# Rows of 512 bytes for W and x, and half of batch 0's x transposed by VectorE

## The reference

```python
x = x + einsum('bnr,bor->bno', einsum('bni,bri->bnr', x, B0[ids]), A0[ids])   # rank 16
base   = einsum('btd,od->bto', x, W)
logits = einsum('btd,ed->bte', x, Wr) + 5.0 * one_hot(lang)
gates  = softmax over the two largest logits, 0 elsewhere
lora   = einsum('bter,bte,eor->bto', einsum('btd,erd->bter', x, A), gates, Bm)
out = x + base + 2.0 * lora
```

## Time and profile before

| | us |
|---|---|
| median of 3 runs (lowest, highest) | 1563.22 (1560.31, 1563.93) |
| profiled execution, its own time | 1561.31 |
| its span, first to last instruction | 1559.5 |
| TensorE busy | 1541.5 |
| VectorE busy | 1230.4 |
| mean granted TensorE clock | 0.996 |

### The profile page before, as it was taken

How to read it: one execution, slowest core, us unless ns; L and a number is a source line. 1 busy time by engine, 2 the same in 40 slices (tenths; PEclk the granted TensorE clock), 3 DMA queues, 4 the chain that set the end, 5 groups by cost and what they waited for, 6 DMA issues and landing times.

```text
span 1559.5 us, 20275 instructions
## 1 busy us (share of the span) xinstructions
PE 1541.5 (99%) x7430; PEld 1298.3 (83%) x7430; DVE 1230.4 (79%) x1692; ACT 714.2 (46%) x911; POOL 79.7 (5%) x119
## 2 busy tenths in 40 slices
PE   9989999999999999999999999999999999999998
PEld 8778878888888888888888888888888888888887
DVE  6998878977799767887688776997769976787665
ACT  6522222544445444455445444454444554445442
POOL 2333331000000000000000000000000000000000
PEclk9999999999999999999999999999999999999999
DMA  9899999787777767687676977667776777666564
GB/s 263 224 276 281 265 254 246 215 230 205 218 231 220 216 196 231 219 229 220 203 224 196 257 207 218 216 205 231 209 218 226 215 217 195 214 219 217 198 219 160
DMA packets 303109, 347.04 MB, mean 223 GB/s; under 512 B 204890, under 2 KB 236682, under 8 KB 302346
## 3 DMA queue, kind: packets, MB, share of 16 engines
q1 hardware_dynamic: 293602, 314.28, 69.8%
q0 software_dynamic: 9136, 30.94, 6.0%
q10 hardware_dynamic: 272, 0.52, 0.1%
HBM read 278.52 MB, written 66.72 MB: 221 GB/s over the span
## 4 chain that ended last, share of the span: by engine, by line
PE 88%; DVE 5%; SPq 4%; DMA 2%; issue 1%; ACT 0%; DVEq 0%; ACTq 0%
PE pb L804 26%; PE pb L805 26%; PE pb L806 26%; PE pb L378 4%; PE pb L380 3%; PE pb L533 2%; SPq L669 2%; SPq L292 2%; DVE raw L684 1%; DVE xl L558 1%; DMA out_dram<-ost 1%; DVE pool_a L540 1%; DMA raw<-in_L_cond_W_dram 0%; DMA an<-in_L_cond_A_dram 0%; PE pb L319 0%
## 5 line engine op out<-in xcount | busy, mean ns | idle before, releaser
L796 ACT CAST wh<-raw 128x1024 fp32r<-128x1024 f32 (+1 forms) x453 | 475.4, 1049 | 705.3 <-PE pb L806 670.9
L800 DVE TENSOR_TENSOR wl<-raw,wh 128x1024 fp32r<-128x1024 f32 (+1 forms) x453 | 552.1, 1219 | 261.3 <-ACT wh L796 260.0
L804 PE MATMUL pb<-wh,sh 128*128 128x512 f32 x1568 | 612.8, 391 | 0.5 <-DVE ost L858 0.5
L805 PE MATMUL pb<-wl,sh 128*128 128x512 f32 x1568 | 611.6, 390 | 0.0
L806 PE MATMUL pb<-wh,sl 128*128 128x512 f32 x1568 | 611.2, 390 | 0.0
L806 PEld LDWEIGHTS pb<-wh,sl 128*128 128x128 f32 x1568 | 294.3, 188 | 62.8
L804 PEld LDWEIGHTS pb<-wh,sh 128*128 128x128 f32 x1568 | 294.5, 188 | 56.2 <-DVE wl L800 0.9
L805 PEld LDWEIGHTS pb<-wl,sh 128*128 128x128 f32 x1568 | 294.6, 188 | 55.1
L378 PE MATMUL pb<-awb,xah 128*128 128x304 f32 x512 | 139.0, 305 | 0.3 <-DVE xal L355 0.3
L380 PE MATMUL pb<-awb,xal 128*128 128x256 f32 x512 | 134.6, 280 | 0.0
L804 PE MATMUL pb<-wh,xh 128*128 128x512 f32 x256 | 101.5, 396 | 0.8 <-DVE xl L558 0.8
(11 more groups left out here) (153 smaller groups left out, 1258.6 us busy)
## 6 DMA issues: line engine op xcount, KB each, us to landing
raw<-t_scr SPq DMA_DIRECT2D x392, 512.0 KB, 4.1
xst<-in_x_dram SPq DMA_DIRECT2D x448, 64.0 KB, 3.8
out_dram<-ost SPq DMA_DIRECT2D x72, 256.0 KB, 3.5
raw<-in_L_cond_W_dram SPq DMA_DIRECT2D x124, 128.0 KB, 5.3
raw<-bt_scr SPq DMA_DIRECT2D x28, 512.0 KB, 3.6
out_dram<-u SPq DMA_DIRECT2D x56, 256.0 KB, 2.9
t_scr<-raw POOLq DMA_DIRECT2D x32, 256.0 KB, 4.4
t_scr<-tst POOLq DMA_DIRECT2D x16, 512.0 KB, 6.7
```

The lines of the kernel that those rows point to most:

```text
L796: e.copy(pair_split(wh, g), pair_source(g)).then_inc(c_wh, 1)
L800: e.tensor_tensor(out=pair_split(wl, g), in0=pair_source(g), in1=pair_split(wh, g).bitcast(f32), op=ALU.subtract).then_inc(c_wl, 1)
L804: e.matmul(o, h, wh[:, g % RING, k, :], start=start, stop=False)
L805: e.matmul(o, h, wl[:, g % RING, k, :], start=False, stop=False)
```

## The change

Rows of W and of x (batches 1 to 7) in DRAM are read 128 floats at a time in place of 64. A load of W is now a "unit" of 256 output rows by 512 inputs (`unit_load`); the two units 2j and 2j + 1 together hold what `w_turn` needs for two W pieces, numbers 2j and 2j + 1, and each `w_turn` reads both. Units rotate through three places: the two `raw` places and the second half of `xst`. Batch 1's x has therefore one place (`x_block` gives `xst` half 0 while n < 2), and `x_load(e, 1, m)` waits until both units of block m - 1 have been turned. Each x block takes four DMAs instead of eight. In VectorE's list the turns of odd W pieces and the pairs of x turns stand ahead of `pair_lo`. For batch 0, blocks m = 1, 3, 5, 7 are loaded with 512-byte rows in four DMAs each and turned by VectorE (`x_turn_first`), which then copies nothing out of PSUM; TensorE keeps m = 0, 2, 4, 6, all copied by ScalarE. The tiles' order of input columns changes with it in A, A0, B0 (same count of instructions, but `columns_turn` is two transposes of half the size).

```diff
-        x_b = x.rearrange("b (h v j) (c k a n) -> b h c k a j v n", h=2, j=32, c=4, k=2, a=4)
-        def x_block(m):
-            return xst[:, m % 2, :, :].rearrange("p t n -> p (t n)")
+        x_b = x.rearrange("b (h v j) (c a n) -> b h c a j v n", h=2, j=32, c=4, a=4)
+        def x_block(n, m):
+            return xst[:, m % 2 if n > 1 else 0, :, :].rearrange("p t n -> p (t n)")
         def x_load(e, n, m, parts=range(4)):
-            if n == 1 and m < 2:
-                if 0 in parts:
+            if n and 0 in parts:
+                if n == 1 and m == 0:
                     e.wait_ge(c_bt, 4)
-            elif n and 0 in parts:
-                e.wait_ge(c_xc, 16 * (n - 1) + 2 * m - 2)
+                elif n == 1:
+                    e.wait_ge(c_xc, 2 * m)
...
-                    for k in range(2):
-                        e.dma_start(x_block(m)[32 * a:32 * a + 32, k * CW:(k + 1) * CW] ...
+                    e.dma_start(x_block(n, m)[32 * a:32 * a + 32, :].rearrange("p (v n) -> p v n", v=8),
+                                x_b[n, half, cols, a]).then_inc(d_x[m % 2 if n > 1 else 0], 16)
+        def x_turn_first(e, u):
+            if u % 2 == 0:
+                e.wait_ge(d_x0[m], 64)
+            e.transpose(two(0, q, kp)..., x_place(m)...[:, u % 2, :, :, :]).then_inc(c_x0[1], 1)
+        def unit_place(n):
+            if n in (2, 3):
+                return xst2[:, n - 2, :, :].rearrange("p t n -> p (t n)")
+            at = n if n < 2 else (n - 1) % 3
+            return (raw[:, at, :, :] if at < 2 else xst[:, 1, :, :]).rearrange("p t n -> p (t n)")
+        def unit_load(e, n):
...
+            elif n > 6:
+                e.wait_ge(c_wc, 4 * ((n - 3) // 2) + 4)
+            for a in range(4):
+                e.dma_start(unit_place(n)[32 * a:32 * a + 32, :]..., raw_w[n // 8, n % 2, n // 2 % 4, a]).then_inc(landed, 16)
         def w_turn(e, g):
-            raw_landed(e, g)
+            for n in range(w // 2 * 2, w // 2 * 2 + 2):
+                unit_landed(e, n)
         def pe_start(e):
-                if s < 12:
+                if s < 12 and (4 + s) // 2 % 2 == 0:
                     x_transpose(e, 4 + s)
         def dve_main(e):
-                if 9 <= i < 25:
-                    x_turn(e, 1, i - 9)
+                if 9 <= i < 25 and i % 2:
+                    for u in range(2):
+                        x_turn(e, 1, i - 9 + u)
+                if turns(i) and w_number(i + 3) % 2:
+                    w_turn(e, i + 3)
...
-                if i + 3 < SLOTS0 and (i + 3) % 9 != 8:
+                if turns(i) and w_number(i + 3) % 2 == 0:
                     w_turn(e, i + 3)
         def sp_main(e):
-                if 10 <= i < 22:
-                    x_load(e, 1, i // 2 - 3, (2, 3) if i % 2 else (0, 1))
-                if i + 5 < SLOTS0 and i != 3:
-                    first_load(e, i + 5)
+                if 10 <= i < 24 and i % 2 == 0:
+                    x_load(e, 1, i // 2 - 4)
+                if turns(i) and w_number(i + 3) % 2 and w_number(i + 3) >= 5:
+                    for n in range(w_number(i + 3) + 2, min(w_number(i + 3) + 4, 32)):
+                        unit_load(e, n)
```

More of the change, by code:

```diff
@@ L197, in adapted_moe_lora_kernel @@
         d_raw = [sem(f"d_raw{n}") for n in range(RAWS)]
+        d_w = [sem(f"d_unit{n}") for n in range(3)]
         d_ts, d_bs = ([sem(f"{name}{n}") for n in range(2)] for name in ("d_ts", "d_bs"))
@@ L616, in w_number @@
             return g // 9 * 8 + g % 9
-        def raw_turn(g):
-            return w_number(g) - (g > 2)
-        def raw_place(g):
-            return raw_turn(g) % 2
-        def raw_in(g):
-            return sum(32 if n == SLOTS0 - 1 else 64 for n in range(g + 1)
-                       if n != 2 and (n % 9 != 8 or n == SLOTS0 - 1) and raw_place(n) == raw_place(g))
-        def raw_before(s):
-            return raw_in(SLOTS0 - 2 + s) if s < 2 else 0
-        def raw_landed(e, g):
-            if g == 2:
-                e.wait_ge(d_w2, 64)
-            elif g in (17, 26):
-                e.wait_ge(d_btx, 32 * (g // 9))
-            else:
-                e.wait_ge(d_raw[raw_place(g)], raw_in(g))
@@ L663, in first_load @@
-            if k == 8:
-                place = btx if g in (17, 26) else raw[:, raw_place(g), 0, :]
-                for w in range(2):
-                    e.dma_start(place[:, w * HT:(w + 1) * HT], bt_scr[:, w, c * HT:(c + 1) * HT]).then_inc(landed, 16)
-            else:
-                for a in range(4):
-                    e.dma_start(w_raw(g)[32 * a:32 * a + 32, :].rearrange("p (g n) -> p g n", g=16), raw_w[c, k, a])\
-                     .then_inc(landed, 16)
+            else:
+                e.wait_ge(c_wc, 60)
@@ L674, in w_turn @@
+            for w in range(2):
+                e.dma_start(gated_place(c)[:, w * HT:(w + 1) * HT], bt_scr[:, w, c * HT:(c + 1) * HT]).then_inc(d_btx, 16)
         def w_turn(e, g):
@@ L1217, in pe_start @@
             small_transpose(e)
-            for u in range(2, 4):
-                x_transpose(e, u)
             for s in range(16):
-                if s < 12:
+                if s < 12 and (4 + s) // 2 % 2 == 0:
                     x_transpose(e, 4 + s)
@@ L1244, in act_start @@
             small_hi(e)
-            x_keep_act(e, 2)
             x_hi(e, 0, 2)
             for s in range(15):
-                if s < 12 and s % 2 == 0:
+                if s < 12 and (4 + s) // 2 % 2 == 0:
                     x_keep_act(e, 4 + s)
@@ L1282, in dve_start @@
             small_lo(e)
-            x_keep_dve(e, 3)
+            for u in (2, 3):
+                x_turn_first(e, u)
             x_lo(e, 0, 2)
             for s in range(15):
-                if s < 12 and s % 2:
-                    x_keep_dve(e, 4 + s)
+                if s < 12 and (4 + s) // 2 % 2:
+                    x_turn_first(e, 4 + s)
                 if s == 8:
@@ L1352, in pool_main, with turns @@
                     bt_difference_store(e)
+        def turns(i):
+            return i + 3 < SLOTS0 and (i + 3) % 9 != 8
         adapter = []
@@ L1389, in sp_start @@
                 e.dma_start(a0g[row:row + R, 0:D].bitcast(f32), (arh, arl)[part][0:R, :]).then_inc(d_ar, 16)
+            for n in range(4, 6):
+                unit_load(e, n)
             for s, t in enumerate((arh, arl)):
                 e.dma_start(a_scr[s, :, 0:D], t).then_inc(d_as, 16)
-            first_load(e, 4)
             e.wait_ge(c_gh, 2)
```

153 lines of the change are left out of this document (94 added, 59 removed).

## The result

The median of four runs of the changed kernel is 1612.3 us (1611.35 to 1613.01), that of the kernel before beside it 1561.76 us: a ratio of 1.0323, 95% interval 1.0305 to 1.0341. It is slower, as I said, but by 50.5 us and not by 7: far outside the range of 1557 to 1577 us that I gave.

The account below looks back on a forecast made before the run. TensorE, busy 99% of the span, was taken as the bound. Start +1.0 and loop +6.5 us on 1561.3 us gave 1568.8, or 1570.7 as a median, stated as 1570 us; range 1557 to 1577 us.

Parts of the forecast that it names:

- VectorE ... gets eight transposes: Batch 0's start: VectorE swaps eight copies of 0.60 us for eight transposes of 0.60 us, so no change.
- x turns of batches 2 to 7 cost the same: Later batches: VectorE's x turns keep their duration and wait for half as many DMAs; no loss.
- the loop's 4 x 0.60 us: Slots 9 to 23: two x turns and one w_turn on VectorE take 2.4 us of each loop.
- The start, +1.0 us, -3.8 to +3.0: Batch 0: TensorE's 3.8 us saving is lost because twelve more x DMAs delay the first W loads; +1.0 us.
- The loop, L = 13.7 us: Slots 9 to 23: turns, W and x issues and landing for batch 1's single x place take 13.7 us per two slots; +6.5 us.
- 7L - 89.4: Loop loss in us after seven loops of length L: nothing up to 12.8 us, then 0.7 us per 0.1 us.
- The output store that holds VectorE's eviction ... I keep it: Near 234 us: TensorE's 2.6 us wait for an eviction stays, between -2.6 and +1.5 us.
- columns_turn, 0.1 us, under cover: Seven times on VectorE: two half-size transposes add 0.1 us each, hidden in the main phase; 0.7 us if not.
- The gates: Batch 0: VectorE's L481 meets GpSimd's large instruction again, so TensorE's 4.4 us wait recurs.
- The clock: 100 to 120 us: granted clock stays at 0.83, 3.4 us of work lost as before; falls elsewhere would show the forecast wrong.
- What was to show it right: Low-part waits of 5 to 8 us together, x turns waiting 2 us or more, first product no earlier than 50 us.
- the lighter queue pays: Rival: halved packets land W and x sooner, start and eviction savings survive; 1556.8 us, chance 0.12.

Follow-up runs that it names:

- e8: Kernel before, with x of batches 1 to 7 and W loaded in 512-byte rows, places and order unchanged: 1562.86 us, ratio 0.9986.
- e9: e8 with one place for batch 1's x, each block requested after both turns of the block before: 1573.3 us, ratio 1.0070.
- e7: e2 with its start undone (batch 0's x in one DMA a block, transposed by TensorE alone): 1585.29 us, ratio 1.0130.
- e11: e7 with batch 0's odd blocks loaded by four DMAs each, TensorE still transposing them: 1586.32 us, ratio 1.0155.
- e2: Changed kernel with all VectorE turns reading 8 bytes apart again in place of 16: 1587.19 us, ratio 1.0157.
- e4: Prices alone, no part of the reference: transposes, copies and additions at several byte steps, x loads in two row sizes; eight turns 4.9 us at 8 bytes, 7.8 at 16.
- e5: e2 with batch 1's x requested ahead of the W units in SP's list: 1580.08 us, ratio 1.0093.
- e10: e7 with batch 1's x requested ahead of the W units in SP's list, the edit of e5: 1576.9 us, ratio 1.0097.
- e1: Kernel before, with VectorE's turns of x and W reading 16 bytes apart in place of 8: 1570.65 us, ratio 1.0052.

## Why the prediction was wrong, step by step

A path from before to after, by the ratios times 1562 us: rows alone -2 (e8); one place for x +13 (e9); W in units of two, with x turned in pairs and the new order of VectorE's list, +9 (e9 to e7); the start's twelve DMAs +4 (e7 to e11, and e2 is the same); reads 16 bytes apart +26 (e2 to the changed kernel). Each part is open by about 4 us, which is as much as the start's whole part. On another path the parts would be other ones: the reads cost 8 us where VectorE has slack.

**"VectorE ... gets eight transposes; two take 1.21 us, so 0.60 each: no change there"; "x turns of batches 2 to 7 cost the same"; the loop's 4 x 0.60 us.** This is the step that failed. I took the duration of a transpose from a row with another access pattern, and never asked what the changed `rearrange` does to the step of the reads. A turn took 0.97 us and not 0.60 (e4: 0.36 us more), and that is worth 26 of the 50 us in the changed kernel (e2). It is not the whole miss: with the turns at the price that I had used, e2 still took 1587 us, outside my range, because the start and the loop, the two terms below, were both sized too small.

**The start, +1.0 us, -3.8 to +3.0.** Measured +8.2 us at the first product, 5.9 with narrow reads. The step named was right, that the first W turn waits for eight DMAs behind twelve more of x (e11 shows it), its size was not. The first W issue was at 24.80 us and not at 22.4, since the x issues there took up to 0.76 us and not 0.5, and the turn that waits for the last load began at 36.44 us, where I had it landed by 33.6. And I had written that VectorE needs it at 31.77 us without looking at what stands behind: two x turns, whose wait ScalarE passes on to TensorE.

**The loop, L = 13.7 us, 7L - 89.4.** Half right. The turns of x came 14.3 us apart in e2 on average (seven intervals from 120.32 to 220.37 us), and 15.6 us apart in the changed kernel (129.38 to 238.43); four turns longer by 0.36 us make 15.1 of my 13.7. By the formula that is +10.7 and +19.8 us. From slot 9 to slot 27 the kernels lost 15.5 and 26.0 us, gaps and clock together. But the mean hides that in the changed kernel loops took from 10.3 to 20.6 us, the longest behind an output store, which my formula didn't have, and that a block could take 7.2 us to land and not 4.6. I gave the W units only a parenthesis, where e5 and e10 show VectorE waiting for them once x is out of the way.

**"The output store that holds VectorE's eviction ... I keep it", 2.6 us.** 6.2 us, and no longer the store: the eviction is queued behind a W turn whose load was late:

```profile
273.82 2.04 DVE L708 STREAM_TRANSPOSE raw<-raw 128x512 f32<-128x512 f32 x2 [3.98 <-DMA raw<-in_L_cond_W_dram]
277.91 1.28 DVE L882 COPY ost<-pb 128x512 f32<-128x512 f32 x2
```

**columns_turn, 0.1 us, under cover.** It isn't covered any more: batches 1 to 6 each lose 0.38 us (47.7 us behind at batch 1's first product, 50.0 at the last), each at one place. In batch 2 VectorE's `pair_lo` (L824) ends there at 524.33 + 1.22 = 525.55 us and TensorE's product starts at 525.61 us, a gap too short for the view of waits; ahead of `pair_lo` stand the two column turns (600 ns each, 419 ns in e2) and an x turn of 1.11 us. It takes both: e1, with long x turns and the old single column turn of 701 ns, has no such drift, and neither has e2.

**The gates** recurred as argued: L503 took 3.10 us beside GpSimd's L1215, and TensorE waited 5.3 us.

**The clock.** I kept the one stretch at 0.83 in 100 to 120 us and named new gaps only as what would make me wrong. Over 0 to 360 us the mean is 0.92 where it was 0.99. By 360 us TensorE is 48 us behind and has been busy 31.5 us less. So of the 48 us 31.5 us are idle time, and at least the other 16 us are work done more slowly. Lower clock alone would make up to (1 - 0.92) x 360 = 29 us, against 4 before, if TensorE had had work all along; part of each low stretch lay beside waits. The low stretches followed gaps, in e9 the one long wait. How much of the loss would stay with the clock held up was not tried.

**What was to show it right** did show up, and was no proof of the size: waits of L402 for VectorE's low parts (16.3 us in seven, not 5 to 8), x turns waiting 3.1, 7.4 and 3.3 us for their DMA, a first product after 50 us. The rival "the lighter queue pays" falls with e8: the queue got 16% lighter per MB, and the time changed by 0.1%, and only 0.3 us of what waited for it before had reached TensorE. The rule of the Trainium skill that I quoted for it ("DMA: Bandwidth & Descriptors", section "Specifications") is not contradicted, but no gain came of it here.

## What to carry to other kernels

When a change rewrites an access pattern, work out the byte step of the innermost reads and writes before taking any duration from the old trace: a row prices an instruction together with its pattern. When it takes a buffer away, write down everything that stands ahead of the new request in its queue, stores included, and everything that will be in flight beside it, and look at the longest such place, not at the mean loop. And don't price an edit apart from the schedule it goes into: the same longer turns cost 8 us in one schedule and 26 us in another.

## What the runs showed of the hardware

VectorE took 4.9 us for eight 128x512 float32 transposes read 4 or 8 bytes apart, 6.0 us at 12 bytes, 7.8 us at 16 and 7.9 us at 32, and 7.4 us when they were written 16 bytes apart (e4). From 8 to 16 bytes additions went from 4.9 to 7.8 us and copies from 2.8 to 4.3 us. TensorE's transposes changed from 272 to 285 ns between 4 and 16 bytes. ScalarE's copies of the same size, one of each, took 619 and 652 ns at 4 and 8 bytes and 1109 and 1128 ns at 16 and 32 (e4). By the busy share of the queue a packet of 512 bytes took 31.5 ns and one of 256 bytes 17.1 ns in e4; in the kernels themselves, with stores beside them, the mean packet of the queue took 36 ns (e8) and 23 ns.
